# Layer 1 of a graph network: the edge transposes of TensorE behind the dense products, and dense stores issued two positions earlier

## What is computed

```python
h = jnp.maximum(_layernorm(x, axis=-1), 0.0)
...
xn = _bn(x, g0, be0)
h = _bn(jax.nn.relu(_gcn_conv(xn, src, dst, edge_weight, W1, b1, n)), g1, be1)
h = _bn(jax.nn.relu(_graph_conv(h, src, dst, edge_weight, Wrel2, brel2, Wroot2, n)), g2, be2)
h = _bn(jax.nn.relu(_graph_conv(h, src, dst, edge_weight, Wrel3, brel3, Wroot3, n)), g3, be3)
...
agg = jax.ops.segment_sum(norm[:, None] * xw[src], dst, num_segments=n)
return agg + xw / deg[:, None] + b
```

## Time and profile before

| | |
|---|---|
| median of 3 runs | 4132.0 us (4131.63 to 4133.24) |
| the profiled execution | 4137.27 us, span 4135.5 us |
| layer 1, first to last dense transpose | 696.1 to 1548.9 us |
| busy over the span | PE 75%, DVE 59%, ACT 45%, POOL 35% |
| HBM traffic over the span | 288 GB/s |

### The profile page before, as it was taken

The page is one execution under the profiler, slowest core; times in us unless marked ns, Lnnn a source line. Parts: engine busy times, 40 slices in busy tenths (PEclk is TensorE's granted clock), DMA queues, the critical chain, the costliest instruction groups (busy, mean ns, idle before and its releaser), DMA issues. The chain is left out here.

```text
span 4135.5 us, 50004 instructions
## 1 busy us (share of the span) xinstructions
PE 3115.6 (75%) x11465; PEld 1891.5 (46%) x11465; DVE 2439.3 (59%) x5239; ACT 1850.5 (45%) x3090; POOL 1430.2 (35%) x1395
## 2 busy tenths in 40 slices
PE   2444443888888883999999999995999999844543
PEld 2444443444444441655655655553444444333432
DVE  4444443777777774888888888783444444433332
ACT  2544452666566661444444444442334444333332
POOL 0332334455555533333333333312222222024344
PEclk8767766999999996999999999997999999955555
DMA  4555553778787775999999999985999999799997
GB/s 129 169 163 179 165 164 117 240 277 282 274 283 283 282 276 171 319 331 346 326 341 340 321 334 336 328 307 184 357 354 353 354 358 354 286 381 380 416 374 308
DMA packets 387808, 1193.34 MB, mean 289 GB/s; under 512 B 61095, under 2 KB 133912, under 8 KB 337570
## 3 DMA queue, kind: packets, MB, share of 16 engines
q1 hardware_dynamic: 282816, 998.32, 65.9%
q0 software_dynamic: 47040, 90.56, 8.9%
q10 hardware_dynamic: 57890, 103.80, 6.6%
HBM read 664.34 MB, written 528.12 MB: 288 GB/s over the span
## 5 line engine op out<-in xcount | busy, mean ns | idle before, releaser
L1000 ACT ACTIVATE l_dn_ho<-l_ps,bias_fold 128x512 f32<-128x512 f32 x588 | 399.2, 687 | 470.0 <-PE l_ps L988 436.3
L1116 POOL DMA_INDIRECT l_ed_gathered<-agg_rows,pos_cols x392 | 403.8, 1030 | 564.0 <-PE l_ps L1151 446.9
L589 PE MATMUL norm_ln_ps<-norm_ln_ho 128*128 128x130 f32 x1568 | 294.4, 372 | 325.3 <-ACT norm_ln_ho L577 324.4
L577 ACT ACTIVATE norm_ln_ho<-norm_ln_x,norm_ln_nbias,norm_ln_rstd 128x128 f32<-128x128 f32 x784 | 306.7, 479 | 294.2 <-DVE norm_ln_nbias L530 256.4
L589 PEld LDWEIGHTS norm_ln_ps<-norm_ln_ho 128*128 128x128 f32 x1568 | 285.0, 284 | 334.9 <-ACT norm_ln_ho L577 333.7
L1123 POOL DMA_INDIRECT l_ed_x_rows<-in_x,dst_cols x196 | 195.5, 997 | 670.6 <-DMA x_dst<-l_ed_x_rows 625.1
L1011 DVE BATCH_NORM_STATS2 bn_stats_all<-l_dn_ho 128x512 f32 (+1 forms) x588 | 370.6, 678 | 80.3 <-ACT l_dn_ho L1000 75.5
L674 PE MATMUL l_ps<-l_dn_columns,w_fold 128*128 128x512 f32 x784 | 379.6, 609 | 47.8 <-ACT l_dn_ho L697 31.8
L988 PE MATMUL l_ps<-l_dn_top,wroot_top 128*128 128x512 f32 x784 | 334.6, 427 | 68.0 <-ACT l_dn_ho L1000 68.0
L503 DVE BATCH_NORM_STATS2 norm_ln_bs<-norm_ln_x 128x6 f32<-128x128 f32 x784 | 192.2, 282 | 297.1 <-DMA norm_ln_x<-in_x 293.5
L697 ACT ACTIVATE l_dn_ho<-l_ps,bias_fold 128x512 f32<-128x512 f32 x392 | 265.1, 687 | 204.9 <-PE l_ps L674 133.7
(11 more groups left out here) (195 smaller groups left out, 5432.0 us busy)
## 6 DMA issues: line engine op xcount, KB each, us to landing
h_dense<-l_dn_ho SPq DMA_DIRECT2D x196, 1024.0 KB, 15.6
l_dn_hi<-h_dense SPq DMA_DIRECT2D x196, 1024.0 KB, 13.5
l_dn_rows<-h_rows SPq DMA_DIRECT2D x98, 520.0 KB
h_rows<-norm_ln_ho SPq DMA_DIRECT2D x97, 520.0 KB, 4.9
l_ed_hd<-h_dst SPq DMA_DIRECT2D x98, 512.0 KB
h_dense<-l_dn_ho SPq DMA_DIRECT2D x98, 512.0 KB, 7.3
out_od_hi<-h_dense SPq DMA_DIRECT2D x98, 512.0 KB
norm_ln_x<-in_x SPq DMA_DIRECT2D x97, 512.0 KB, 4.2
```

Of the source, the lines that this page charges most:

```text
L577: ins = act.activation(ho[:, j, g, 0:C], xt[:, j, g, :], ACT.Relu, bias=nb[:, j, g:g + 1], scale=rs[:, j, g:g + 1])
L589: ins = pe.matmul(ps[:, 0, 0:TC], ho[0:rows, j, g, 0:C], ho[0:rows, j, g, :], start=first and g == 0, stop=final and g == G - 1, skip_grou ...
L1000: act.activation(ho[:, j, m, c * CW:(c + 1) * CW], ps[:, u % 2, 0:CW], ACT.Relu, bias=bf[:, m:m + 1]).then_inc(rl[j], 1)
L1116: pool.indirect_dma_start(tg[:, j, g, :], None, tab[n - 1][:, :], bass.IndirectOffsetOnAxis(ap=pos_c[:, t:t + 1], axis=0)).then_inc(gat[j] ...
```

## The change

PE's two `turn` stages become works of their own, listed behind both others. PE's list in a step is then: `table` or `dst`, `spread`, dense `products`, edge `turn`, dense `turn`; before it was `table` or `dst`, `spread`, edge `turn`, `products`, dense `turn`. No lag changes on PE, and no wait. On SP the dense store's lag goes from 8 to 6; the list's order stays.

```diff
-                return NS, [(0, load), (8, store)], end
+                return NS, [(0, load), (6, store)], end
 
             def tensor(pe):
-                def turn(i, j):
...
-                return NS, [(5, products), (3, turn)], None
+                return NS, [(5, products)], None
+
+            def tensor_turn(pe):
+                def turn(i, j):
...
+                return NS, [(3, turn)], None
...
-            return dict(sync=sync, tensor=tensor, scalar=scalar, vector=vector)
+            return dict(sync=sync, tensor=tensor, scalar=scalar, vector=vector), dict(tensor=tensor_turn)
...
-                return HALVES, [(6, chunk(table, 0)), (6, chunk(dst, 1)), (4, chunk(spread)), (2, chunk(turn))], None
+                return HALVES, [(6, chunk(table, 0)), (6, chunk(dst, 1)), (4, chunk(spread))], None
+
+            def tensor_turn(pe):
...
+                return HALVES, [(2, chunk(turn))], None
...
-            side_by_side(ph, DI, [edge_rows(ph, ps), dense_rows(ph, ps)])
+            edges, edges_turn = edge_rows(ph, ps)
+            dense, dense_turn = dense_rows(ph, ps)
+            side_by_side(ph, DI, [edges, dense, edges_turn, dense_turn])
```

More of the change, by code:

```diff
@@ L675, in products @@
                                   start=True, stop=True).then_inc(mm[j], 1)
-                return NS, [(5, products), (3, turn)], None
+                return NS, [(5, products)], None
+            def tensor_turn(pe):
+                def turn(i, j):
+                    wait_use(pe, msk[j], i)
+                    i1, j1 = before(i, j, 1, NS)
+                    for c in range(CH):
+                        wait_use(pe, ev[j1], i1, CH, c + 1)
+                        for g in range(EG):
+                            ins = pe.transpose(ps[:, c, g * P:(g + 1) * P], ht[:, j, c * EG + g, 0:C], ident[:, :])
+                        ins.then_inc(tu[j], 1)
+                return NS, [(3, turn)], None
             def scalar(act):
@@ L807, in tensor @@
             def tensor(pe):
[L808 to L817, removed]
                 def spread(i, j, part):
@@ L851, in dst, with turn @@
                         pe.matmul(o, w1[:, 0, m * C:(m + 1) * C], xd[:, j, :], start=False, stop=True).then_inc(mm_d[j], 1)
-                return HALVES, [(6, chunk(table, 0)), (6, chunk(dst, 1)), (4, chunk(spread)), (2, chunk(turn))], None
+                return HALVES, [(6, chunk(table, 0)), (6, chunk(dst, 1)), (4, chunk(spread))], None
+            def tensor_turn(pe):
+                def turn(i, j, part):
+                    if part == 0:
+                        wait_use(pe, gat[j], i, 16 * 2 * EG)
+                        i1, j1 = before(i, j, 1, ES)
+                        wait_use(pe, ev[j1], i1, 2)
+                    else:
+                        wait_use(pe, ev[j], i, 2, 1)
+                    for g in range(EG):
+                        ins = pe.transpose(ps[:, TURN, g * P:(g + 1) * P], (ts, td)[part][:, j, g, 0:C], ident[:, :])
+                    ins.then_inc(tu[j], 1)
+                return HALVES, [(2, chunk(turn))], None
             def scalar(act):
@@ L930, in edge_rows @@
                 stood[j] += 16 * 2 * EG * uses(ES, j)
-            return dict(sync=sync, gpsimd=gpsimd, tensor=tensor, vector=vector, scalar=scalar)
+            return dict(sync=sync, gpsimd=gpsimd, tensor=tensor, vector=vector, scalar=scalar), dict(tensor=tensor_turn)
         def dense_layer(ph, n, kb, mb, h_in, h_out, ps):
```

## The result

The median went from 4131.8 to 4064.5 us (4 runs each; 4054.5 to 4076.0 after), a ratio of 0.9839 with an interval of 0.9811 to 0.9866: 67 us less, where 114 were predicted. All ratios here are formed from the fast runs; of all runs in this document one, of `e1_order_only`, is a slow one (4200.6 us). The profiled execution's span is 4065.4 us, against 4135.5. Of these 70 us layer 1 holds 56: the aggregate behind it begins at 1519.6 instead of 1575.6. Layer 2, whose code is unchanged, takes 1234.6 instead of 1245.6 us from there to the next aggregate; the executions profiled on other chips, of either kernel and of its variants, lie between 1231 and 1244, so I count these 11 us as variation, not as the change's. Behind layer 2 no part moves by more than 3 us.

A forecast was written before the change was run, and what follows sets the result against it. No unit is full in layer 1; who waits for whom, seen on PE, decides. (1.55 + 1.09) x 46 + 2 = 123 us, cut to 114 for DMA and late rows: 4018 us; forecast 4004 to 4032 (62%), wider 4002 to 4075 (81%).

The forecast's parts named there:

- Products ahead of the edge transposes: Layer 1, PE: the 1.01 us wait before edge transposes goes, a shorter ReLU wait comes; 1.55 us a pair saved.
- Dense store two positions earlier: Layer 1, SP: stores issued about 15 us sooner, so ACT's ReLU no longer waits for them; 1.09 us a pair saved.
- The end of the layer: Layer 1's last SP issues: the final dense store comes two positions earlier; 2 us saved.
- DMA: Layer 1: engines 92% busy in a 14.89 us pair, some loads late; with late rows, pair taken at 15.1.
- Late rows: Layer 1, POOL and DVE: gathers start 2.9 us later, coefficients 2 to 5 us late; covered, but by little.
- The sign: Layer 1, profile after: PE idle ahead of `spread`, its message late, would show the margin gone; no size given.
- DMA takes over in part: Rival, layer 1: loads and stores queue longer, DVE or ACT waits; pair 15.9, 77 us saved, 4055; 20%.
- Gathers set the pace: Rival, layer 1: later, longer POOL gathers make a pair of 18.8, 58 us slower, 4190; 5%.

The follow-up runs named there:

- e1: The changed kernel with the dense store back at lag 8, so only PE's new order: 4164.8 us, 1.019 of the kernel before on the same chip.
- e2: The kernel before with only the dense store moved to lag 6, PE's order old: 4035.7 us, 0.991 of the kernel before on the same chip.
- e7: The changed kernel with the dense store at lag 7 instead of 6: 3992.8 us, 0.980 of the kernel before on the same chip.
- e3: The changed kernel with DVE's coefficients moved behind sums, self loop and statistics: 3944.8 us, 0.969 of the kernel before on the same chip.
- e6: e5 with DVE's coefficients also moved behind sums, self loop and statistics: 3915.0 us, 0.960 of the kernel before on the same chip.
- c1: The changed kernel unedited, run again on the second experiment chip: 3996.8 us, 0.980 of the kernel before there.
- e4: The changed kernel without gathers of destination rows from the third chunk on: 3938.4 us, 0.967 of the kernel before on the same chip.
- e5: The changed kernel with the edge transposes between the second and third product: 3926.5 us, 0.963 of the kernel before on the same chip.
- c0: The kernel before unedited, profiled again on the second experiment chip: 4079.6 us, one run.

## Why the prediction was right, and where it fell short

*Products ahead of the edge transposes, 1.55 us a pair: right, slightly small.* Undisturbed pairs fell from 16.4 to 14.70, 1.7 us; the third product waits 0.27 us in the even step shown, not the 0.33 of the earlier trace rows. What the prediction didn't say is that this term stands only together with the other. By itself the order was +97 us (e1).

*Dense store two positions earlier, 1.09 us a pair: right.* Alone it left a pair of 16.48 against the 16.44 forecast. In time it gave 32 us where 50 had been expected; what the other 18 are isn't shown, since the kernel before has no profile on that chip, and e2's four runs lie 12 us apart. One position would have done (e7).

*The end of the layer, 2 us:* neither shown nor refuted; it is too small beside the 11 us that layer 2 varied by.

*DMA: the deduction wasn't needed.* At 0.92 it was to cost some of the 0.21 us a pair. e3 had a share of 0.92 with a pair of 14.81:

```profile
740.00:1340.00 600.00, 571.76 (x2353) 305.60 (x2353) 500.20 (x934) 420.54 (x693) 351.22 (x325) 1.00 0.92 330
```

and e6 0.98 with one of 13.87, at the same 4.9 MB a pair (330 x 14.81 and 352 x 13.87). By the Trainium skill, page "DMA: Bandwidth & Descriptors", section "Specifications", HBM gives about 358 GB/s to a core: the sustained 352 of e6 lie below it, the 396 of a short stretch above it.

*Late rows: the step that failed.* The prediction wrote: "First to miss it would be the second spread of the chunk, which needs DVE's message one step later; on my count it is there some 2 us ahead of need." It followed who uses the rows. It didn't ask what else stands in DVE's list behind the wait for them. The self loop does, and the first spread of the same step needs it. The prediction's own numbers leave nothing there: with a landing of 3 us its coefficients come 17.5 + 3 - 14.89 = 5.6 us behind the start of the pair's second spread, and 1.43 us on to the next first spread is 7.0; but in the trace above that spread is due 1034.40 - 0.55 - 1027.44 = 6.4 us behind it. With no margin, each landing that takes longer than usual is paid by PE. The sign, idle time of PE ahead of `spread`, stands in the prediction, but put down to a late message. This cost 38 us in c1, where the rows show it place by place; e3 and e4, on the other chip, and e6 against e5 on the same, are nearly without it, by the order of DVE alone or by fewer gathers. That is shown. In the run that was predicted, on the first chip, PE's waits for the self loop are 11.1 us.

*The long odd steps, 47 us on the first chip: PE's semaphore updates came late, why is open.* The prediction had no term for it. They are the larger part of the 77 us there, and no experiment could reach them, since they didn't occur on the chips of the experiments: c1, the same kernel, has none, and its gain was 81 us where the first chip's was 67. Releases of this kind are in the first profile of the kernel before as well, outside this stage (ACT's L577 in the norm, 32.0 us in 3), so they are not made by the change. Whether they strike a step more when the margins are thin isn't known.

The forecast proper, a pair of 14.8 to 15.4 us and 4004 to 4032, was missed: the pair was 16.37 and the time 4064.5. That the time lies inside 4002 to 4075 it owes to the room left for DMA, which was not the cause; so far that is luck.

Of the rivals, "DMA takes over in part" named a pair of 15.9 and 4055 us, which is near the time that came, and for another reason: what queued wasn't transfers but DVE's list behind one of them. "Gathers set the pace" fell: POOL still waits 262.8 us for PE's edge transposes in the layer.

## What to carry to other kernels

When a step is shortened or moved, list for each engine what stands in its in-order list behind every wait that becomes later, and who needs it, write-after-read on a bank included; the first to suffer is often not a user of the late data. Put the instruction that waits for the latest arrival last in its engine's list. Two edits of which each makes the other's wait shorter or longer can't be priced apart: here one alone was 97 us worse, the other 32 better, and with a further one-line change all of it was 123 better.

## What was new of the hardware

- Behind a PE stall of 3.45 us the granted clock was 0.50 in the next 5 us, and two products took 3.78 us instead of 1.98 (e1). Until the clock was back this cost 2.7 us, nearly as much as the wait.
- Every fourteenth block of eight gathers has a gap on POOL, 2.25 us in c1 where 0.30 is usual. In c1 the coefficients of chunks 14, 28 and 42 (counted from 0) came 6.5 to 6.9 us behind the last gather, where 2.5 to 3.7 is usual and a few others have 4.8 to 5.6; their blocks took 11.7 to 12.7 us, and these three chunks made 22 of the 38 us. In the kernel before such blocks, 12.7 us long, lie 245 us apart, at 910, 1156 and 1401, fourteen pairs too, but their rows aren't late (2.6 us and less), nor are they in the changed kernel's first profile (3.3 and less). So the gap is regular, the lateness isn't. What comes round after 112 gathers the trace doesn't say.
- A gather takes 0.95 us, and over 1.3 only if it starts while DVE runs an op that reads two SBUF tiles: in c1 40 of 42 beside the scan (L917), 6 of 73 beside L714 and 4 of 27 beside L925, but none of 41 beside L908, one of whose inputs is PSUM, and none anywhere else.
- On one chip, and not on the two others, PE's semaphore updates came up to 5 us behind the end of the work that they tell of, several in a row some 0.05 us apart, and all engines that waited for them went on together.
- The kernel before takes 4132 us on one chip and 4068 to 4080 on two others; layer 1 begins 25 us earlier there, and the output is 16 us shorter (c0).
